# Moving three element-wise steps of a block quantiser from GpSimd to VectorE, and deepening the queue of pending attention matmuls

## The reference, cut to what matters

```python
x = x + 0.5 * ffn(layernorm(x), weight, bias)
x = x + attn(layernorm(x), Wq, Wk, Wv, W_G, W_O)
x = x + 0.5 * ffn(layernorm(x), weight, bias)

def ffn(x, weight, bias):            # both operands quantised in blocks of 32
    xq, xs = mx_quantize(x)          # scale = max|block| / 7.5, values on the FP6 E2M3 grid
    wq, ws = mx_quantize(weight)
    return (xq * xs) @ (wq * ws).T + bias

def attn(x, ...):                    # 8 heads of width 128, sequence 2048
    scores = q @ k.T / sqrt(128);  ret = (scores * decay) @ v     # decay is causal
    ret = (ret - mean) * rsqrt(var + 1e-6)
    return (silu(x @ W_G) * ret) @ W_O
```

## Time and profile before

| | |
|---|---|
| median of 2 timed runs | 1867.98 us (1867.88 to 1868.08) |
| time of the profiled execution | 1866.38 us |
| its span (slowest core, core 5) | 1864.7 us |
| spans of the 8 cores | 1858.7 to 1864.7 us, mean granted TensorE clock 0.73 on every core |
| busy: PE / DVE / ACT / POOL | 823.9 / 917.7 / 540.4 / 301.9 us (44 / 49 / 29 / 16 %) |

### The profile page before, as it was taken

One profiled execution on the slowest core, in us unless ns is written; L12 is line 12 of the kernel. 1 busy time (PEld: TensorE's weight loads), 2 busy tenths in 40 slices (PEclk: granted clock), 3 DMA queues, 4 the chain that ended last, 5 costly groups with the idle time before them and its releaser, 6 DMA issues.

```text
span 1864.7 us, 15515 instructions; the slowest of 8 cores (1858.7 to 1864.7 us)
## 1 busy us (share of the span) xinstructions
PE 823.9 (44%) x3904; PEld 357.2 (19%) x3904; DVE 917.7 (49%) x1169; ACT 540.4 (29%) x1414; POOL 301.9 (16%) x173
## 2 busy tenths in 40 slices
PE   0010033444460657859694455554429204443445
PEld 0000011111110223324242233332214101111111
DVE  2878677666640223330104454544433166677663
ACT  0443322222218600003234444444420632222220
POOL 0333232233220100000000000000001013433333
PEclk9999986565565578879796777776669655666556
DMA  7100100000000454440200000000034200000000
GB/s 226 34 22 0 46 0 1 0 0 0 1 1 12 169 181 147 170 151 8 68 1 1 1 1 1 1 1 1 1 113 119 85 0 23 22 23 34 22 23 34
DMA packets 19044, 81.28 MB, mean 44 GB/s; under 512 B 2192, under 2 KB 2192, under 8 KB 16656
## 3 DMA queue, kind: packets, MB, share of 16 engines
q1 hardware_dynamic: 11904, 53.02, 8.5%
q0 software_dynamic: 7056, 27.27, 4.0%
HBM read 61.41 MB, written 18.87 MB: 43 GB/s over the span
## 4 chain that ended last, share of the span: by engine, by line
PE 40%; DVE 25%; ACT 14%; issue 11%; DMA 6%; POOL 1%; SPq 1%; DVEq 1%; ACTq 1%; POOLq 0%
PE psc L60 32%; DVE arena L60 25%; ACT arena L60 14%; PE pt L60 4%; PE pbig L60 4%; POOL arena L60 1%; DMA arena<-wo 1%; DMA arena<-wf 1%; DMA arena<-wq 1%; DMA arena<-wv 1%; DMA arena<-wk 1%; SPq L60 1%; DMA arena<-wg 1%; DVEq L68 1%; ACTq L68 1%
## 5 line engine op out<-in xcount | busy, mean ns | idle before, releaser
L60 PE MATMUL psc<-arena 128*128 128x512 bf16 (+1 forms) x2240 | 637.4, 437 | 134.5 <-DVE arena L60 114.8
L60 PE MATMUL pt<-arena 128*128 128x128 bf16 x576 | 137.7, 263 | 893.9 <-ACT arena L60 639.1
L60 POOL TENSOR_TENSOR arena<-arena 128x1024 f32<-128x1024 f32 (+1 forms) x120 | 272.3, 2269 | 644.6 <-DVE arena L60 631.1
L60 DVE TENSOR_SCALAR arena<-arena 128x1024 f32<-128x1024 f32 (+4 forms) x348 | 237.3, 682 | 238.5 <-ACT arena L60 177.0
L60 PEld LDWEIGHTS psc<-arena 128*128 128x128 bf16 (+1 forms) x2240 | 224.6, 106 | 471.1 <-issue 309.6
L60 DVE SCALAR_TENSOR_TENSOR arena<-arena 128x1024 f32<-128x1024 f32 (+3 forms) x211 | 246.2, 1167 | 29.1 <-ACT arena L60 8.3
L60 PEld LDWEIGHTS pt<-arena 128*128 128x128 bf16 x576 | 60.0, 104 | 983.9 <-issue 972.7
L60 ACT ACTIVATE arena<-arena 128x1024 f32<-128x1024 f32 (+2 forms) x187 | 184.2, 986 | 145.6 <-DVE arena L60 136.9
L60 ACT CAST arena<-arena 128x1024 int32<-128x1024 f32 x40 | 41.8, 1045 | 548.8 <-DVE arena L60 548.8
L60 ACT COPY arena<-pt 128x128 bf16<-128x128 bf16 x576 | 139.0, 265 | 181.5 <-PE pt L60 167.1
L60 ACT CAST arena<-psc 128x512 bf16<-128x512 f32 (+1 forms) x224 | 106.0, 496 | 292.2 <-PE psc L60 249.5
(11 more groups left out here) (15 smaller groups left out, 144.9 us busy)
## 6 DMA issues: line engine op xcount, KB each, us to landing
arena<-x SPq DMA_DIRECT2D x4, 2048.0 KB, 21.0
xspill<-arena POOLq DMA_DIRECT2D x16, 512.0 KB, 2.9
arena<-qsc SPq DMA_DIRECT2D x8, 1024.0 KB, 4.9
arena<-ksc SPq DMA_DIRECT2D x8, 1024.0 KB, 4.8
arena<-xspill POOLq DMA_DIRECT2D x16, 512.0 KB, 3.8
out<-arena POOLq DMA_DIRECT2D x16, 512.0 KB, 3.1
arena<-wf SPq DMA_DIRECT2D x8, 512.0 KB, 3.4
arena<-wq SPq DMA_DIRECT2D x8, 512.0 KB, 4.4
```

The source lines that it names most:

```text
L60: inst = getattr(getattr(self.nc, eng), name)(*a, **k)
```

## The change

The three GpSimd operations of `q_gq` become the last three operations of a single VectorE function `q_B2`; the semaphore `gq` and all waits on it go. `q_B1` keeps the step size in the one buffer `qb2` and works in a separate `rb_buf`, so its first two operations no longer have a wait between them. `q_B2` puts one of the two corrections in a buffer of its own, `cm_buf`, so that two of its operations have no wait between them either. TensorE's transposes and `x_d` now wait for VectorE's count. In the heads `pending` holds three blocks back instead of two.

```diff
-        def q_B1(p, yy_s, k, q_g):
-            sbuf = s_par[k % 2]
+        def q_B1(p, yy_s):
             c.wait("vector", "s", yy_s)
-            c.wait("vector", "gq", q_g)
-            c.op("vector", "tensor_scalar", sbuf, qb1, 4.0, 0.125,
+            c.op("vector", "tensor_scalar", qb2, qb1, 4.0, 0.125,
                  ALU.is_ge, ALU.mult).inc("v")
-            c.wait("vector", "v")
-            c.op("vector", "tensor_scalar", qb1, qb1, 16.0, 0.25,
+            c.op("vector", "tensor_scalar", rb_buf, qb1, 16.0, 0.25,
                  ALU.is_ge, ALU.mult).inc("v")
...
-        def q_B2a(p, cast_s, scratch, sc_guard_g):
+        def q_B2(p, cast_s, scratch, out_bf, xd_guard_t):
             c.wait("vector", "s", cast_s)
             c.wait("vector", "v")
-            c.wait("vector", "gq", sc_guard_g)
+            if xd_guard_t:
+                c.wait("vector", "t", xd_guard_t)
             c.op("vector", "scalar_tensor_tensor", scratch, qbi, -1.0,
                  qby_y[p], ALU.mult, ALU.add).inc("v")
             c.wait("vector", "v")
             c.op("vector", "tensor_scalar", qby_y[p], scratch, 0.5, None,
                  ALU.is_gt).inc("v")
-            c.wait("vector", "v")
-            c.op("vector", "tensor_scalar", scratch, scratch, -0.5, -1.0,
+            c.op("vector", "tensor_scalar", cm_buf, scratch, -0.5, -1.0,
                  ALU.is_le, ALU.mult).inc("v")
             c.wait("vector", "v")
-            c.op("vector", "scalar_tensor_tensor", qby_y[p], qbi, 0.0,
+            c.op("vector", "scalar_tensor_tensor", scratch, qbi, 0.0,
                  qby_y[p], ALU.bypass, ALU.add).inc("v")
+            c.wait("vector", "v")
+            c.op("vector", "tensor_tensor", scratch, scratch, cm_buf,
+                 ALU.add).inc("v")
+            c.wait("vector", "v")
+            c.op("vector", "tensor_tensor", scratch, scratch, qb2,
+                 ALU.mult).inc("v")
+            c.wait("vector", "v")
+            sclb = q_scl2[p].unsqueeze(2).broadcast_to([128, 32, 32])
+            c.op("vector", "tensor_tensor", b32(out_bf), b32(scratch), sclb,
+                 ALU.mult).inc("v")
             return c.cnt["v"]
-
-        def q_gq(p, k, na_v, scratch, out_bf, tr_guard_t):
...
-                c.wait("tensor", "gq", xxd[k])
+                c.wait("tensor", "v", xxd[k])
...
-                    x_d(rc + 2, xna[rc - 1] if rc >= 1 else xy[rc],
-                        xxd[rc - 1] if rc >= 1 else 0)
+                    x_d(rc + 2, xxd[rc - 1] if rc >= 1 else xy[rc])
...
-                    if len(pending) > 2:
+                    if len(pending) > 3:
                         emit_ret(*pending.pop(0))
```

More of the change, by code:

```diff
@@ L31 @@
 ENGS = ("sync", "vector", "scalar", "tensor", "gpsimd")
-SEMS = ("ld", "g", "v", "s", "t", "gq", "wa", "wb", "ga", "gb")
+SEMS = ("ld", "g", "v", "s", "t", "wa", "wb", "ga", "gb")
 class _I:
@@ L269, in q_yy @@
             return c.cnt["s"]
-        def q_B1(p, yy_s, k, q_g):
-            sbuf = s_par[k % 2]
+        def q_B1(p, yy_s):
             c.wait("vector", "s", yy_s)
-            c.wait("vector", "gq", q_g)
-            c.op("vector", "tensor_scalar", sbuf, qb1, 4.0, 0.125,
+            c.op("vector", "tensor_scalar", qb2, qb1, 4.0, 0.125,
+                 ALU.is_ge, ALU.mult).inc("v")
+            c.op("vector", "tensor_scalar", rb_buf, qb1, 16.0, 0.25,
                  ALU.is_ge, ALU.mult).inc("v")
             c.wait("vector", "v")
-            c.op("vector", "tensor_scalar", qb1, qb1, 16.0, 0.25,
-                 ALU.is_ge, ALU.mult).inc("v")
-            c.wait("vector", "v")
-            c.op("vector", "scalar_tensor_tensor", sbuf, sbuf, 0.125, qb1,
+            c.op("vector", "scalar_tensor_tensor", qb2, qb2, 0.125, rb_buf,
                  ALU.add, ALU.add).inc("v")
             c.wait("vector", "v")
-            c.op("vector", "tensor_scalar", qb1, qb1, 24.0, 12.0,
+            c.op("vector", "tensor_scalar", rb_buf, rb_buf, 24.0, 12.0,
                  ALU.mult, ALU.add).inc("v")
             c.wait("vector", "v")
-            c.op("vector", "scalar_tensor_tensor", qb1, sbuf, -32.0, qb1,
+            c.op("vector", "scalar_tensor_tensor", rb_buf, qb2, -32.0, rb_buf,
                  ALU.mult, ALU.add).inc("v")
             c.wait("vector", "v")
-            c.op("vector", "tensor_tensor", qby_y[p], qby_y[p], qb1,
+            c.op("vector", "tensor_tensor", qby_y[p], qby_y[p], rb_buf,
                  ALU.mult).inc("v")
@@ L307, in q_B2a @@
                  ALU.is_gt).inc("v")
-            c.wait("vector", "v")
-            c.op("vector", "tensor_scalar", scratch, scratch, -0.5, -1.0,
+            c.op("vector", "tensor_scalar", cm_buf, scratch, -0.5, -1.0,
                  ALU.is_le, ALU.mult).inc("v")
             c.wait("vector", "v")
-            c.op("vector", "scalar_tensor_tensor", qby_y[p], qbi, 0.0,
+            c.op("vector", "scalar_tensor_tensor", scratch, qbi, 0.0,
                  qby_y[p], ALU.bypass, ALU.add).inc("v")
-            return c.cnt["v"]
-        def q_gq(p, k, na_v, scratch, out_bf, tr_guard_t):
[L317 to L329, removed]
+            c.wait("vector", "v")
[8 more added lines that the diff above has]
+                 ALU.mult).inc("v")
+            return c.cnt["v"]
         def transpose_1024(src_bf, dst_fn):
@@ L347, in ffn_sublayer @@
                 ln_tail(EPS_LN)
-            global qby_y, s_par
+            global qby_y, rb_buf, cm_buf
             if build_wdt:
                 qby_y = [qby, qb3]
-                s_par = [qb2, qb0]
+                rb_buf = qb0
+                cm_buf = qb0
                 wy = {}; wyy = {}; wtq = {}; wcast = {}; wxd = {}
@@ L367, in w_B2 @@
                 def w_B2(k):
[L368 to L371, removed]
+                    xg = wtr[k - 2] if k >= 2 else 0
+                    wxd[k] = q_B2(k % 2, wcast[k], ffntmp, wdrow_sb[k % 2], xg)
                 def w_tr(k):
-                    c.wait("tensor", "gq", wxd[k])
+                    c.wait("tensor", "v", wxd[k])
                     transpose_1024(wdrow_sb[k % 2],
@@ L386, in ffn_sublayer @@
                     c.wait("vector", wsem, dma_here[jc])
-                    c.wait("vector", "gq", wxd[jc - 2] if jc >= 2 else 0)
                     wy[jc] = q_stageA(jc % 2, wst_sb[jc % 2], None)
@@ L391, in ffn_sublayer @@
                         w_B2(jc - 1)
-                    wtq[jc] = q_B1(jc % 2, wyy[jc], jc,
-                                   wxd[jc - 2] if jc >= 2 else 0)
+                    wtq[jc] = q_B1(jc % 2, wyy[jc])
                     wcast[jc] = q_cast(jc % 2, wtq[jc])
@@ L413, in ffn_sublayer @@
             db = [qb0, wst_sb[1]]
-            s_par = [qb2, wst_sb[0]]
+            rb_buf = wst_sb[0]
+            cm_buf = wst_sb[0]
             sd = {}; xy = {}; xyy = {}; xtq = {}; xcast = {}; xxd = {}
-            xna = {}
             tr_done = {}
@@ L419, in ffn_sublayer, with x_d @@
             mm_done = {}
-            def x_d(rc, guard_v, guard_g=0):
+            def x_d(rc, guard_v):
                 c.wait("scalar", "v", guard_v)
-                if guard_g:
-                    c.wait("scalar", "gq", guard_g)
                 c.op("scalar", "activation", db[rc % 2], x_sb[:, rc, :],
@@ L429, in x_B2 @@
             def x_B2(k):
[L430 to L435, removed]
+                xg = tr_done[k - 2] if k >= 2 else 0
+                xxd[k] = q_B2(k % 2, xcast[k], db[(k + 1) % 2],
+                              xdrow_sb[k % 2], xg)
             def x_tr(k):
-                c.wait("tensor", "gq", xxd[k])
+                c.wait("tensor", "v", xxd[k])
                 s_after = transpose_1024(
@@ L489, in ffn_sublayer @@
                 c.wait("vector", "s", sd[rc])
-                c.wait("vector", "gq", xxd[rc - 2] if rc >= 2 else 0)
                 xy[rc] = q_stageA(rc % 2, db[rc % 2], ln_rstd[:, rc:rc + 1])
@@ L496, in ffn_sublayer @@
                     ffn_evac(rc - 2)
-                xtq[rc] = q_B1(rc % 2, xyy[rc], rc,
-                               xxd[rc - 2] if rc >= 2 else 0)
+                xtq[rc] = q_B1(rc % 2, xyy[rc])
                 xcast[rc] = q_cast(rc % 2, xtq[rc])
                 if rc + 2 < RC:
-                    x_d(rc + 2, xna[rc - 1] if rc >= 1 else xy[rc],
-                        xxd[rc - 1] if rc >= 1 else 0)
+                    x_d(rc + 2, xxd[rc - 1] if rc >= 1 else xy[rc])
                 if rc >= 1:
```

## The result

| | kernel before | changed kernel |
|---|---|---|
| median of all runs | 1867.39 us (8 runs) | 1807.58 us (9 runs) |
| ratio | | 0.968, 95% interval 0.967 to 0.969 |
| profiled execution, its span | 1866.38 us, 1864.7 us | 1807.58 us, 1806.1 us |
| spans of the 8 cores | 1858.7 to 1864.7 us | 1799.9 to 1806.1 us |

The change makes the kernel 3.2% faster, by 60 us.

A forecast was written before the change was run, and what follows sets the result against it. The bound was taken to be rings of waits through several engines, with POOL's work mostly hidden. Weight stage 18.5, feed-forward steps 23.6 and heads 4.8 sum to 46.9 us gained, forecasting 1821 us, range 1810 to 1835.

The forecast's parts named there:

- the stretch: Quantiser rows: DVE operations run longer while POOL works, q_B1 6.19 us without POOL against 9.77 in a steady weight row.
- the choice between the two pages of the Trainium skill: Start-up rows: POOL also slows two-input DVE instructions, not only two-port modes; the narrower rule makes the sum 5.8 us smaller.
- Weight rows: Weight stage: DVE becomes the bound at 17.90 us against 20.15 a row; 18.5 us gained in the stage.
- the 3.99 for the new operations: DVE, each row: three operations taken over from POOL at 1.33 us each, including 0.10 us to the next start.
- Feed-forward rows: Both feed-forward steps: 19.65 us behind a fast matmul group, 22.0 behind a slow one, 5 of 13 slow; 23.6 us gained.
- the ring through TensorE: Feed-forward row: evacuation, q_B1, cast, transposes, matmuls, next evacuation; about 19.1 to 22.1 us by matmul group, against DVE's 19.46.
- Heads: Attention heads: three blocks held back issue the last scores one product earlier; 0.3 us a half, 4.8 us in 16 halves.
- The clock: Rival, feed-forward matmuls: a lower TensorE clock takes back a good part of the gain, 1836 to 1862 us; chance 0.15.
- the full version: Clock rival's extreme: every feed-forward matmul group at 0.50 clock, all rows 22.1 us, total gain 6.6 us, 1861 us.
- The deeper queue: Rival, heads: the fourth pair of scores waits 0.5 us for slots, losing 8 us instead of gaining 4.8; 1834 us; chance 0.06.
- The quantiser terms: Forecast gains outside the heads: 18.5 us in the weight stage and 23.6 us in the two feed-forward steps.
- its 4 us for the last rows of the steps: Ends of the feed-forward steps: 4 us of possible gain, left out of the sum but used for the range's 1810 end.

The follow-up runs named there:

- the move alone: Changed kernel with the queue back at two blocks and both removed waits restored, leaving three operations moved from GpSimd to VectorE: 1823.16 us, ratio 0.972.
- both fusions: Changed kernel with q_B2's rounding correction in two operations instead of four and q_B1 in four instead of six: 1679.37 us; repeated 1682.49 us, ratio 0.897.

## Why the prediction was right in its mechanism and short in its size

- **POOL's work was hidden, the gain is the stretch.** Right. The run with idle work on POOL shows the stretch as contention, on both kinds of instruction, and the choice between the two pages of the Trainium skill came out as the row had said.
- **Weight rows: DVE becomes the bound at 17.90 us.** The bound right, the size too long by 0.59: 17.31. This is the first mis-sized step: "the two waits that go I cost at nothing", with the ends at nothing and 0.1 us. A removed wait is worth 0.20 us, twice a row; putting both back costs 3.1 us of this stretch (158.4 against 155.3). The third piece is in the 3.99 for the new operations: the last of them has no wait behind it, and `q_B1` starts 3.80 us after the first of them (89.17 to 92.97). The rows of before showed the price: the evacuation at 336.61, with no wait on it, is followed by the next operation after 1.14 us and not 1.33, and so is `q_B1`'s last operation by the reduction. I read 0.10 us from the gap between the end of one and the start of the next, which is not what a wait costs. Six rows at 0.59 make 3.5 us, and the difference between 21.9 and 18.5 is 3.4.
- **Feed-forward rows: bound by the ring through TensorE, DVE's new work in its idle time.** Right, and the run with the shorter `q_B2` shows it. The mean row came out at 20.53 us against 20.55 forecast, by luck, as errors cancel: half of the groups are of the long kind, not 5 in 13, but a row with one takes 21.5 to 21.6 us, not 22.0, as its group takes 8.7 and not 9.0 and the pair 0.2 less, and one with a short group 19.43, not 19.65. The steps gained 12.4 and 14.1 us against 11.8. The removed waits have no part in that, since the steps are as long with them (333.6 and 333.3 us against 333.8 and 333.4, means of eight cores); in the second step it is the start, which before began with a group of 9.0 us and now with one of 6.6.
- **Heads: 0.3 us a half, at most 0.41.** The step that failed most: 0.6 us, 9.7 us over 15 halves on the cores shown and 10.6 to 10.8 in the device time. I took the 0.41 us at the last six products for all there was to win, but that wait is still there. What went is a wait of 0.22 us one group earlier, and 0.22 us of products moved from ahead of the last scores to behind them. These two make 0.44. The rest goes with TensorE's granted clock. Between the first and the last scores of a half (all cores, without the first half) the clock was at its lower level, 1.2 GHz, for 3.9 us before, 3.3 in the changed kernel and 3.5 with the deeper queue in the kernel before. With that time counted half, the stretch falls from 8.0 us to 7.6 in both, which is the 0.4 above, and the shorter time at the low level gives the other 0.2 to 0.3. Why that time gets shorter no run shows.
- **The rivals.** The clock did take back a part, as half of the groups are long; no run has all of them long, so the price of the full version is untested. The deeper queue did not cost anything. The quantiser terms of the sum, 18.5 + 23.6 = 42 us, were nearly met by the run with the move alone, 44 us.
- **The range** ended at 1810 us because both ends of the queue (0 and 0.41 us a half) and of the waits (0 and 0.1 us) were set below the measured values. Both were taken from one place of the trace, not from the difference between two places where only that thing differs. That 1810 is near the time at all owes something to its 4 us for the last rows of the steps, which did not come: from the fourteenth to the last evacuation of the first step it is 30.3 us before and after.

## What to carry to other kernels

A wait that is always met still has a price (0.20 us here between two DVE operations), so independent operations should stand next to each other, and the price can be read from the starts of two neighbours with and without a wait. It counts where that engine is the bound (3 us over the weight rows) and counted nothing in the feed-forward rows. Element-wise work on GpSimd is not free for VectorE even if nobody waits for it: look for one shape with two durations in VectorE's rows and put POOL's rows beside them. What counts in a ring of engines is the part up to the hand-over (here `q_B1` up to the cast), and shortening the rest of the same engine's work gives nothing until it becomes the bound.

## What had not been expected of the hardware

Contention is mutual, and the two engines take turns. GpSimd's additions rose from 2.36 to 3.19 us each (mean of 120) when VectorE read two tensors from SBUF at the same time. Single operations from the run with work for POOL:

```profile
101.63 3.32 POOL L60 TENSOR_TENSOR arena<-arena 128x1024 f32<-128x1024 f32 x1 [13.48 <-DVE arena L60]
102.86 3.18 DVE L60 TENSOR_TENSOR arena<-arena 128x1024 f32<-128x1024 f32 x1
105.10 3.14 POOL L60 TENSOR_TENSOR arena<-arena 128x1024 f32<-128x1024 f32 x1
```

POOL's first ends at 104.95 and DVE's at 106.04, 1.09 us later, which is about what it takes alone (1.22). POOL's second ends at 108.24, 2.20 us after DVE's, again about its 2.36 alone. So in these rows neither operation seems to advance while the other works.

The groups of 20 matmuls after nearly equal pauses ran at mixed clocks, 6.2 us or 8.7, in strict alternation over most of a step, where before about one in three was long, and the share changed from kernel to kernel (10 of 32 before, 16 of 32 after, 14 with the waits put back, 9 with both fusions). The spacing of the rows alone does not set it: in the run with work for POOL nearly all rows are 23.8 us apart, and 6 groups of the first step are long but 14 of the second. Between a long and a short group lie 2 to 3 us, so as an estimate this share alone can move such a kernel by 10 us. It can also hide a change: with the waits put back the mean feed-forward row stays at 20.5 us, since fewer groups are long.
